# A graph-attention layer: `f2` by rows stored as its 32x32 blocks come, and the signs written with a step of four bytes

## The reference

```python
in_fts = W @ inlayer.T
f1 = (w1 @ in_fts).T + b1
f2 = (w2 @ in_fts).T + b2
logits = f1 + f2.T
bias_mat = jnp.where(adj_mat > 0, 0.0, NEG_INF)
coefs = jax.nn.softmax(jax.nn.leaky_relu(logits) + bias_mat, axis=-1)
vals = coefs @ inlayer
x = _layernorm(x + vals, axis=-1)
```

## Time and profile before

| | us |
|---|---|
| median of 3 runs | 274.48 |
| lowest, highest | 274.23, 276.32 |
| profiled execution | 275.19 |
| its span | 273.5 |
| granted clock of TensorE, mean | 0.997 of full |

### The profile page before, as it was taken

The page is one execution under the profiler, slowest core; times in us unless marked ns, Lnnn a source line. Parts: engine busy times, 40 slices in busy tenths (PEclk is TensorE's granted clock), DMA queues, the critical chain, the costliest instruction groups (busy, mean ns, idle before and its releaser), DMA issues.

```text
span 273.5 us, 5997 instructions
## 1 busy us (share of the span) xinstructions
PE 258.2 (94%) x2195; PEld 225.6 (82%) x2195; DVE 242.6 (89%) x309; ACT 195.6 (72%) x296; POOL 67.2 (25%) x98
## 2 busy tenths in 40 slices
PE   2999988799999999999999999999999999999991
PEld 2989877688888888888888888888888888888880
DVE  2888999988888899999999999999998999999963
ACT  2479999949999996999199919991999198003140
POOL 4002046930000006300630063006300630054150
PEclk9999999999999999999999999999999999999998
DMA  6999999999999999999999999999999999801011
GB/s 196 256 298 309 311 313 282 285 272 311 313 315 318 315 314 315 323 339 315 316 324 342 318 316 280 361 328 327 240 335 309 309 285 337 226 2 38 0 49 31
DMA packets 22562, 73.64 MB, mean 269 GB/s; under 512 B 3090, under 2 KB 4244, under 8 KB 22548
## 3 DMA queue, kind: packets, MB, share of 16 engines
q1 hardware_dynamic: 11184, 35.17, 42.9%
q10 hardware_dynamic: 9956, 34.64, 42.0%
q0 software_dynamic: 1408, 3.67, 4.7%
HBM read 71.37 MB, written 2.10 MB: 269 GB/s over the span
## 4 chain that ended last, share of the span: by engine, by line
DVE 58%; PE 16%; issue 8%; ACT 7%; DMA 7%; DVEq 1%; ACTq 1%; POOL 1%; POOLq 0%
DVE mn L743 19%; PE ps L1091 16%; DVE msk L756 11%; DVE mn L748 11%; DMA nat<-in_adj 5%; DVE post L855 3%; ACT sgn L474 3%; DVE ybt L870 2%; DVE bns L875 2%; ACT bt L542 2%; DVE ntot L860 2%; DVE post L857 2%; ACT post L518 2%; DMA msk<-in_x 2%; DVE mv L879 1%
## 5 line engine op out<-in xcount | busy, mean ns | idle before, releaser
L1091 PE MATMUL ps<-bt,msk 128*128 128x258 f16 x2048 | 232.1, 274 | 3.6 <-DVE msk L756 2.7
L1091 PEld LDWEIGHTS ps<-bt,msk 128*128 128x128 fp8e5 x2048 | 200.5, 98 | 34.2 <-issue 4.6
L474 ACT ACTIVATE sgn<-f2b,nf1l 128x1024 int8<-128x1024 f32 x128 | 136.4, 1144 | 5.2 <-POOL flag L409 4.0
L743 DVE TENSOR_SCALAR mn<-nat 128x4096 int8<-128x4096 int32 x32 | 73.1, 2284 | 5.0 <-DMA nat<-in_adj 4.6
L416 POOL TENSOR_SCALAR nmr<-mv 128x4 f32<-128x4 f32 x7 | 12.8, 1835 | 143.5 <-DVE mv L879 143.5
L756 DVE STREAM_TRANSPOSE msk<-mn 128x1024 uint32<-128x1024 uint32 x32 | 39.8, 1245 | 2.6
L748 DVE SCALAR_TENSOR_TENSOR mn<-sgn,mn 128x1024 uint32<-128x1024 uint32 x32 | 39.2, 1225 | 3.0 <-ACT sgn L474 2.0
L623 ACT ACTIVATE ybt<-ybt,nmr,rstd 128x128 f32<-128x128 f32 x28 | 11.5, 483 | 38.7 <-POOL nmr L421 38.7
L616 ACT ACTIVATE post<-ps,ac 128x258 f32<-128x258 f32 x60 | 24.8, 467 | 10.9 <-PE ps L1091 10.9
L761 DVE TENSOR_SCALAR msk<-msk 128x1024 uint32<-128x1024 uint32 x32 | 22.2, 695 | 1.0
L427 POOL DMA_DIRECT2D out<-ybt x24 | 13.7, 572 | 16.3 <-ACT ybt L623 14.9
(11 more groups left out here) (115 smaller groups left out, 105.2 us busy)
## 6 DMA issues: line engine op xcount, KB each, us to landing
nat<-in_adj SPq DMA_DIRECT2D x64, 512.0 KB, 15.1
nat<-in_adj ACTq DMA_DIRECT2D x64, 512.0 KB, 17.6
xn<-in_x POOLq DMA_DIRECT2D x4, 512.0 KB, 19.8
out<-ybt POOLq DMA_DIRECT2D x24, 64.0 KB, 6.6
msk<-in_x SPq DMA_DIRECT2D x8, 128.0 KB, 4.2
msk<-in_x ACTq DMA_DIRECT2D x8, 128.0 KB, 4.5
out<-ybt SPq DMA_DIRECT2D x4, 64.0 KB, 1.8
out<-post SPq DMA_DIRECT2D x4, 32.0 KB, 2.4
```

The source lines that it names most:

```text
L474: ins = act.activation(sgn[:, c, g * JA:(g + 1) * JA], f2b[:, :], ACT.Sign, bias=nf1l[:, bass.ds(G * t + g, 1)], scale=-1.0)
L743: dve.tensor_scalar(mn[:, c % 2], nat[:, c], 0, EDGE, ALU.is_gt, ALU.mult).then_inc(cast_done, 1)
L1091: ins = pe.matmul(ps[:, 2 * c + m, 0:2 * DV], mask_f[c][m][:, n // KB, n % KB, :], btv[m][:, n, :], start=(n == 0), stop=(n == NK - 1))
```

## The change

`f2b` is stored in the order b, k, r in place of b, r, k. `f2_rows` then writes its 32x32 blocks one behind the other, in a run, where it wrote words 16 bytes apart. The signs keep their place in memory: ScalarE reads `f2b` in a run, as before, and writes through a pattern of 8 x 4 x 32 bytes whose innermost step is four bytes, where it wrote 1024 bytes in a run. The fallback branch reads `f2b` through a pattern with a step. The program is otherwise the same, with the same instructions in the same order on every engine and the same waits.

```diff
             def signs(t, c, between=None):
                 for g in range(G):
-                    ins = act.activation(sgn[:, c, g * JA:(g + 1) * JA], f2b[:, :], ACT.Sign,
+                    ins = act.activation(sgn[:, c, g * JA:(g + 1) * JA].rearrange("p (b r k) -> p b k r", r=SQ, k=KB),
+                                         f2b.rearrange("p (b k r) -> p b k r", r=SQ, k=KB), ACT.Sign,
                                          bias=nf1l[:, bass.ds(G * t + g, 1)], scale=-1.0)
...
             def f2_rows():
-                dve.transpose(f2b.rearrange("p (b r k) -> p b k r", r=SQ, k=KB),
+                dve.transpose(f2b.rearrange("p (b k r) -> p b k r", r=SQ, k=KB),
                               f2l.rearrange("p (b k o) -> p b k o", k=KB, o=1).to_broadcast([P, NB, KB, SQ])
                               ).then_inc(f2b_ready, 1)
...
                     pe.matmul(ps[:, j % 2, :], ident[:, a * SQ:a * SQ + 1].to_broadcast([P, P]),
-                              f2b[:, half * 512:(half + 1) * 512], start=True, stop=True).then_inc(g_f2_made, 1)
+                              f2b.rearrange("p (b k r) -> p b r k", r=SQ, k=KB)[:, half * NB // 2:(half + 1) * NB // 2], start=True, stop=True).then_inc(g_f2_made, 1)
```

## The result

| | kernel before | changed kernel |
|---|---|---|
| median of 4 runs, us | 274.36 | 278.73 |
| lowest, highest | 274.02, 276.32 | 278.20, 279.29 |
| profiled execution, its span | 275.19, 273.5 | 278.20, 276.5 |

The ratio is 1.0152, with a 95% interval of 1.012 to 1.0185. The forecast was 274.5 us in a range of 273.4 to 277.0; the time lies outside it.

What follows compares the result with a forecast made beforehand. TensorE was 94% and VectorE 89% busy, VectorE holding 58% of the chain. Signs 0 plus transpose 0 (hidden) left the median at 274.5 us, range 273.4 to 277.0, with rival 3 left out.

Steps and rivals of the forecast that it cites:

- The transpose, 2023 to about 1245 ns: VectorE's transpose that writes `f2b` (L702): writing one run shortens it to about 1245 ns, saving 0.78 us.
- the 0.78 us are hidden: Ahead of the first cast on VectorE: the transpose's saving only lengthens the wait for the adjacency transfer; gain 0.
- I take the f32 rows: 0 us for each sign: ScalarE's 128 signs: f32 writes at the same addresses show no extra cost, so 0 us in all.
- Rival 2: ScalarE's signs: each partly written 16-byte stretch costs 4.0 ns, a sign grows 0.17 us, 275.9 us in all; 12%.
- 8 signs are on the path: Ahead of the loop, 8 signs stand in the chain at full length; at 0.17 us each, 1.4 us reach the end.
- A sign may get longer by 0.29 us before ScalarE has no idle time left: Main loop, 52.42 to 228.80 us: ScalarE's 32.1 us of idle time shared among 112 signs.
- Rival 3: ScalarE's signs: narrow stepped writes slow for each element, making ScalarE the bound; 338 to about 640 us; 18%.
- Rival 1: VectorE ahead of the first cast: the transpose's 0.8 us gain reaches the end, 273.7 us; 5%.
- the neighbours: VectorE's reads of the signs (L748) stay at 1225 ns, unharmed by more store traffic of ScalarE.

Runs made afterwards that it cites:

- the transpose alone: `f2_rows` writes `f2b` in a run as in the change, signs written as in the kernel before; 0.9977 of the kernel before.
- the kernel with short rows: Kernel before with `f2b` in its old order, signs reading and writing 32 rows of 32 elements without a step; 1.003 of the kernel before.
- The probe: Kernel before plus three activations of each output form behind its last store, into a dead buffer; int8 with a step of four took 1395 ns, no ratio.
- the step alone: Signs written with the step of four as in the change, `f2b` written as in the kernel before; 1.0129 of the kernel before.
- the loop-only kernel: Changed kernel with the 16 signs ahead of the loop written in a run, only the loop's 112 with the step; 1.016 of the kernel before.
- the two kernels shown: Changed kernel with the step only in the 16 signs of tiles 0 to 3, or only in the loop's 112; 1.0135 and 1.016 of the kernel before.
- the planes: Apparently `f2b` in the order k, b, r, signs writing 4 rows of 256 bytes with a step of four; 1.0149 of the kernel before.
- both kernels with a copy: Step only in the first tiles' signs, or only in the loop's, with GpSimd copying `f2b` to a second tensor; 1.0098 and 1.0211 of the kernel before.

## Why the prediction was wrong, point by point

- **The transpose, 2023 to about 1245 ns:** right, 1235. That the 0.78 us are hidden: the transpose alone gave 0.9977 with 1 inside its interval, so not contradicted, and not shown to the last tenth. The cover was another than forecast. The wait for the transfer ahead of the first cast was to grow from 0.58 to 1.36 us; in the changed kernel there is none (the cast starts at 20.77), with the transpose alone it is 0.40. The time is gone before that, at L728 (L727 before), where VectorE's wait for TensorE's matmul of the statistics grows from 0.29 to 0.98 us. In the kernel with short rows, whose transpose still takes 2.03 us and whose first sign starts at the same time as in the change, that copy starts at 20.41, in the change at 20.40.
- **The signs, "I take the f32 rows: 0 us for each sign":** this is the step that failed. The f32 rows have the right addresses and the wrong width. The probe gives 1132 ns for f32 there and 1395 for int8. The argument that "the width of the element is not what the engine pays for" was drawn from runs, in which narrow elements fill their words. The row that had both, narrow and with a step, was L511, and I judged it by its addresses.
- **Rival 2, the price per partly written stretch, 12%:** the right mechanism. It put a stretch at 4.0 ns; it is 4.4, and since only the excess over the elements' own time counts, that raised 0.17 us for a sign to 0.25 or 0.26.
- **"8 signs are on the path":** afterwards the chain passes through 12. The chain shows only what was last before. Tile 0's four signs had 0.85 us of room ahead of the combine (they end at 23.47 us, the combine waits for the cast until 24.32), and on ScalarE the wait of 0.55; 4 x 0.25 us more used both up. So 8 x 0.17 = 1.4 us became 8 x 0.25 and 0.3 of tile 0, the 2.3 us of the kernel with the step alone. The change had 3.1, with 0.8 from the stalled issue of a transfer, which no term of the sum had.
- **"A sign may get longer by 0.29 us before ScalarE has no idle time left":** a mean over 176 us. From 58.16 to 95.56 us ScalarE was busy in the kernel before 37.39 of 37.40 us; the idle time lay later. In that stretch the longer signs push back the eviction that TensorE needs at tile 8, and in the loop-only kernel, with that eviction first, the loss went from 1.6% to 0.26%. It does not show in the total on top of the first delay, because the two run beside each other; the prediction saw neither, so nothing in it earned that.
- **Rival 3, ScalarE as the bound element by element:** not so. The chain does pass through ScalarE up to 98 us, but what holds TensorE there is the eviction's place in the order, and the price is one for each stretch.
- **Rival 1 and the neighbours:** L748's 1225 ns (L749 now) held. TensorE was taken as a given; its half clock after a pause was not thought of.
- **The rule of the Trainium skill (SBUF — State Buffer, Specifications)** that two accesses to a 16-byte line are enough for full bandwidth: the runs agree for f32 words (four to a line free, one to a line dearer) and contradict it for bytes and halves of words: with four accesses to a line a sign takes 1395 ns, with two 2522. The prediction read the rule as silent on elements narrower than a word. That holds for the entry it cites; in its note on SBUF cachelines the same page does extend it to them, and the rows above contradict that too. The measurement decides.

The chances given to "slower" were 0.20. Nearly all of that lay on rival 3, which did not come; rival 2, which has the mechanism, was put at 0.5% and inside the range.

## What to carry to other kernels

Judge a new access pattern by a row that has the same element width and the same way of filling words, not only the same addresses: four bytes at a step of one word are not a word. A slack that is a mean over a long stretch says nothing about its first part; cut the stretch where the work piles up. And where an engine writes ahead for one reader and clears buffers for another in one order, its longer instructions hit the second: look at who stands behind them.

## What the runs showed of the hardware

- ScalarE, writes of 1 or 2 bytes that leave words partly written: 4.4 to 4.9 ns for each visit to a 16-byte stretch, hidden where the elements in it take longer (8 elements: 1135 ns against 1131; 4 elements: 1395).
- ScalarE, full f32 words one to a stretch of 16 bytes: 2049 ns for 1024, against 1132 in a run. VectorE's transpose with words 16 bytes apart: 2023 ns against 1235.
- TensorE, after 3.2 to 3.4 us without a matmul: granted clock 0.50 (1.2 GHz) for some 2.5 to 3.5 us in the two kernels shown, and starts 214 to 218 ns apart in the profiled executions of four more (the step alone, the planes, both kernels with a copy); the full clock at once in that of the change.
